# One lap loop for all rounds, the product with the one-hot columns behind the next step's sums, and the short block first, in a GNN layer on one Trainium2 core

## The chip, the cores and the metric

The kernel runs on one core of one Trainium2 chip. The metric is the device time of one execution in microseconds; the median of three runs is given. Engines are named as in the profile: PE (TensorE matmul), PEld (its weight loads), DVE (VectorE), ACT (ScalarE), POOL (GpSimd), SP (SyncE). q1 is the DMA queue that SP issues on, q10 the one of ACT.

## What is computed

```python
agg = segment_sum(edge_attr, dst, num_segments=6250)     # 200000 edges x 128 features, float32
h = relu(concatenate([x, agg, u[0]], axis=1) @ W1 + b1)  # x: 6250 x 128
y = x + h @ W2 + b2
out = (y - mean(y)) / sqrt(var(y) + 1e-5)                # by row
```

dst is sorted. The edges are 102 MB, x and the output 3.2 MB each.

## The kernel before

**Steps.** The edges are cut into 65 steps of 3072 (1.5 MB each), taken from the last to the first, plus a rest of 320 edges. Step t lands in one of 5 slots by one DMA on SP (line 304); SP issues load t when level1 of step t - 5 is done (level1_done). From t = DENSE = 30 on, a partition reads 12 edges in a row (wide form), before that 6.

**The sums of a step.** level1 (line 798) is 96 small products of PE: one-hot matrices `hot` (32 columns, made by DVE in make_hot, three steps ahead) times edges, into rows_ps, a PSUM buffer. ACT copies rows_ps to the SBUF buffer rows (copy_rows, line 412). level2 (line 815) multiplies rows by `row_hot`, a second one-hot matrix, into cols_ps; DVE adds cols_ps to agg_t at the step's base (add, line 602) and so frees the single cols_ps. There are three pairs of rows_ps and rows, used in the order SETS.

**The laps.** 5 steps are a lap, 13 laps in all, and a lap finishes one block of 512 nodes (the last of them 128 nodes, `final`). In laps 0 to 5 (sparse_lap) the columns are 224 and PE does level1(t), then level2(t - 1). In laps 6 to 12 (dense_lap) they are 128, and PE does level1(t), then level2(t), which waits for ACT's copy of the same step. These are two loops, with their own code on PE and DVE; SP, ACT and POOL are written out step by step.

**The block's layer.** For the block of lap l: turn_x (four transposes of x_rows into turn_ps, which is the same bank as hid_ps), copy_x (ACT), product1_x, product1_agg (after the last add of the lap), relu (ACT), product2, residual, variance, reciprocal_deviation (POOL), normalise, store. All but the turns come in the lap after. POOL's bias_add reads x_rows; then ACT issues the next x load. Block 11 (`short`) holds nodes 128 to 511 and the last 106 nodes, in three DMAs. In the last lap PE does a dummy product (line 903) ahead of level1(64).

**The judge.** In lap 8 DVE looks through all indices (judge, line 648), in lap 9 it makes `plan`, which says whether the general path must run.

## Time and profile before

| | us |
|---|---|
| median of three runs | 278.71 (277.7 to 279.08) |
| the profiled execution | 279.02 |
| its span | 277.3 |
| PE busy in the span | 215.6 (78%) |
| DVE busy | 168.1 (61%) |
| ACT busy | 51.3 (19%) |
| POOL busy | 41.5 (15%) |
| read from and written to memory | 106.63 MB, 3.20 MB |

The busy times are of one execution, taken by the hardware profiler; its own time stands beside its span. Ends of matmuls are modelled, so distances between starts say more than durations. A high busy share says nothing yet about who is waited for.

### The profile page before, as it was taken

The numbers are of one execution on the slowest core, as the hardware profiler recorded it, in microseconds if no ns is written. First come the engines' busy times: TensorE is split into PE (matmuls) and PEld (weight loads), VectorE is DVE, ScalarE is ACT, GpSimd is POOL, SyncE is SP. The second block draws the span as 40 slices with busy tenths as digits, with TensorE's granted clock in tenths as the row PEclk, the third lists the DMA queues.
The fourth block names the chain that finished last, engine by engine and source line by source line (L and its number), as shares of the span: only waits on it lengthen the run. The fifth ranks groups of instructions, "written<-read, shape, count | busy, mean of one in ns | idle before, by whom it ended". The sixth has DMA issues, their size and how long they took to land.

```text
span 277.3 us, 15287 instructions
## 1 busy us (share of the span) xinstructions
PE 215.6 (78%) x6763; PEld 171.2 (62%) x6763; DVE 168.1 (61%) x425; ACT 51.3 (19%) x100; POOL 41.5 (15%) x49
## 2 busy tenths in 40 slices
PE   0997599987776786796877599895897996867872
PEld 0895487856655665575556368674776675655751
DVE  7932475793774665665772526959938768464542
ACT  0511022311211210220210211322022122121210
POOL 6400020030210300400400300300304012030020
PEclk9999989999999999999995979999599999999998
DMA  7999999999999999999999999999999999999994
GB/s 248 351 386 400 401 398 400 401 401 402 402 399 402 402 400 401 402 400 412 417 412 409 416 414 418 414 417 416 417 415 418 414 419 414 409 423 410 420 399 175
DMA packets 30623, 110.06 MB, mean 397 GB/s; under 512 B 1976, under 2 KB 3150, under 8 KB 30606
## 3 DMA queue, kind: packets, MB, share of 16 engines
q1 hardware_dynamic: 27508, 105.83, 96.0%
q10 hardware_dynamic: 3098, 4.00, 4.1%
q8 instruction: 10, 0.16, 0.2%
q14 instruction: 7, 0.06, 0.1%
HBM read 106.63 MB, written 3.20 MB: 396 GB/s over the span
## 4 chain that ended last, share of the span: by engine, by line
PE 56%; DMA 18%; issue 15%; DVE 7%; POOL 1%; ACT 1%; DVEq 0%; POOLq 0%; ACTq 0%
PE rows_ps L810 30%; DMA slots<-in_edge_attr 18%; PE cols_ps L822 14%; PE hid_ps L854 3%; PE hid_ps L836 3%; PE hid_ps L845 2%; PE hid_ps L830 1%; ACT rows L418 1%; PE hid_ps L938 1%; DVE first_of_pair L540 1%; POOL rstd L382 1%; DVE dst_local L550 1%; DVE high L650 1%; DVE lowest L651 1%; DVE stats L630 1%
## 5 line engine op out<-in xcount | busy, mean ns | idle before, releaser
L810 PE MATMUL rows_ps<-slots,hot 64*32 64x128 f32 x6240 | 113.4, 287 | 34.3 <-issue 28.9
L810 PEld LDWEIGHTS rows_ps<-slots,hot 64*32 64x32 f32 x6240 | 94.4, 111 | 51.5 <-issue 49.6
L608 DVE TENSOR_TENSOR agg_t<-agg_t,cols_ps 128x128 f32 (+1 forms) x65 | 21.6, 332 | 94.8 <-PE cols_ps L822 94.7
L822 PE MATMUL cols_ps<-row_hot,rows 128*128 128x128 f32 (+1 forms) x260 | 56.8, 343 | 13.9 <-ACT rows L418 6.3
L582 DVE TENSOR_TENSOR hot<-edge_node,iota 128x768 f32<-128x768 f32 x65 | 61.9, 952 | 2.1 <-issue 1.8
L822 PEld LDWEIGHTS cols_ps<-row_hot,rows 128*128 128x128 f32 x260 | 41.2, 200 | 28.3 <-issue 15.1
L418 ACT ACTIVATE rows<-rows_ps 128x256 f32<-128x256 f32 x65 | 25.0, 384 | 179.4 <-PE rows_ps L810 175.4
L382 POOL TENSOR_TENSOR rstd<-var_eps,minus_half 128x4 f32<-128x4 f32 (+1 forms) x13 | 16.6, 1276 | 201.9 <-DVE var_eps L639 201.9
L598 DVE TENSOR_TENSOR row_hot<-row_node,iota 128x256 f32<-128x256 f32 (+1 forms) x65 | 38.5, 592 | 0.0
L373 POOL TENSOR_TENSOR z<-x_rows,b_all 128x512 f32<-128x512 f32 (+1 forms) x13 | 17.2, 1323 | 28.0 <-PE hid_ps L830 27.9
L645 DVE TENSOR_SCALAR z<-z,moments,rstd (+1 forms) x49 | 17.4, 412 | 1.1 <-POOL rstd L382 1.0
L438 ACT ACTIVATE x_t<-hid_ps 128x512 f32<-128x512 f32 (+2 forms) x13 | 13.1, 1011 | 8.4 <-PE hid_ps L830 8.4
L854 PE MATMUL hid_ps<-w_sb,hid 128*128 128x128 f32 x98 | 13.9, 283 | 0.5 <-ACT hid L449 0.5
L836 PE MATMUL hid_ps<-x_t,w1x 128*128 128x512 f32 (+1 forms) x26 | 13.4, 596 | 0.5 <-DVE agg_t L608 0.5
L854 PEld LDWEIGHTS hid_ps<-w_sb,hid 128*128 128x128 f32 x98 | 12.3, 191 | 2.0 <-issue 1.4
L449 ACT ACTIVATE hid<-hid_ps,bias 128x512 f32<-128x512 f32 (+2 forms) x13 | 8.5, 654 | 22.6 <-PE hid_ps L845 21.1
L845 PE MATMUL hid_ps<-agg_t,w1a 128*128 (+1 forms) x24 | 11.8, 574 | 0.5 <-DVE agg_t L608 0.5
L630 DVE BATCH_NORM_STATS2 stats<-z 128x6 f32 (+1 forms) x49 | 10.7, 279 | 0.0
L620 DVE TENSOR_TENSOR z<-z,hid_ps 128x512 f32 (+1 forms) x13 | 8.5, 653 | 1.6 <-PE hid_ps L854 1.6
L830 PE MATMUL hid_ps<-ident,x_rows 128*128 128x128 f32 x49 | 7.7, 276 | 0.8 <-issue 0.2
L845 PEld LDWEIGHTS hid_ps<-agg_t,w1a 128*128 128x128 f32 x24 | 4.4, 189 | 5.5 <-issue 4.7
L830 PEld LDWEIGHTS hid_ps<-ident,x_rows 128*128 128x128 f32 x49 | 5.7, 140 | 2.7 <-issue 2.4
(111 smaller groups left out, 65.6 us busy)
## 6 DMA issues: line engine op xcount, KB each, us to landing
slots<-in_edge_attr SPq DMA_DIRECT2D x65, 1536.0 KB, 17.3
x_rows<-in_x ACTq DMA_DIRECT2D x11, 256.0 KB
out<-z SPq DMA_DIRECT2D x11, 256.0 KB
dst_int<-in_dst SPq DMA_DIRECT2D x1, 384.0 KB, 3.8
dst_int<-in_dst ACTq DMA_DIRECT2D x1, 384.0 KB, 4.7
x_rows<-in_x ACTq DMA_DIRECT2D x1, 192.0 KB
out<-z SPq DMA_DIRECT2D x1, 192.0 KB
rest_slot<-in_edge_attr ACTq DMA_DIRECT2D x1, 160.0 KB, 8.8
```

The costliest lines, as they stand in the source:

```text
L373: G.tensor_tensor(z[:, bass.ds(i, 1), 0:m, :].rearrange("p o r f -> p (o r) f"), x_rows[:, 0:m, :], b2_all[:, :].unsqueeze(1).broadcast_to ...
L382: G.tensor_tensor(rstd[:, 0:m], var_eps[:, 0:m], minus_half[:, 0:m], ALU.pow).then_inc(rstd_made, 1)
L418: A.activation(rows[i][:, :, :], rows_ps[i][:, :, 0:feats], ACT.Copy).then_inc(rows_copied, 1)
L582: V.tensor_tensor(hot[i][:, :, :], edge_node[:, bass.ds(t, 1), :, :].rearrange("p o c r -> p (o c r)").unsqueeze(2).broadcast_to([P, RUNS, ...
L598: V.tensor_tensor(row_hot[i][:, :, 0:n], row_node[:, bass.ds(t, 1), :].rearrange("p o h -> p (o h)").unsqueeze(2).broadcast_to([P, HALVES, ...
L608: V.tensor_tensor(cols, cols, cols_ps[:, 0:n], ALU.add).then_inc(added, 1)
L645: done = V.tensor_scalar(row(i, r), row(i, r), moments[:, r, 0:1], rstd[:, r:r + 1], ALU.subtract, ALU.mult)
L810: done = T.matmul(rows_ps[i][c * SPAN:(c + 1) * SPAN, h, 0:feats], hot[j][part, c * RUN + r, :], slots[part, j, c, r * feats:(r + 1) * fea ...
L822: done = T.matmul(cols_ps[:, 0:n], rows[i][:, h, :], row_hot[j][:, h, 0:n], start=(h == 0), stop=(h == HALVES - 1))
L836: T.matmul(hid_ps[:, 0:n], w1x[:, :], x_t[:, 0:n], start=True, stop=False)
L845: done = T.matmul(hid_ps[:, 0:n], w1a[:, :], agg_t[:, bass.ds(at, n)], start=False, stop=True)
L854: done = T.matmul(y_ps[:, r, :], hid[:, r * P:(r + 1) * P], w2_sb[:, :], start=True, stop=True)
```

## The change

- One loop runs over laps 0 to 12 on PE and over laps 1 to 12 on DVE (lap 0 is written out there, and DVE's pass begins with the last step of the lap before). All steps but the last have 224 columns, and level2(t - 1) comes behind level1(t), except at j = 4 (the last step of a lap), where level2(t - 1) comes ahead of level1(t), because steps 3 and 4 of a lap use the same pair of buffers.
- There are two pairs of rows_ps and rows. The turned x gets a PSUM bank of its own (turn_bank), and the small products of the start move to it and to few_ps.
- product1_x moves from the start of the next lap to j = 4 of its own lap, behind turn_x (j = 3) and level2 of step 3. product1_agg is at j = 1, product2 at j = 2. turn_x and product1_x always take four tiles of rows.
- The blocks now begin at node 128. The first one is the short one (490 nodes, 122 partitions of four rows and one of two), in three DMAs; POOL zeroes x_rows before. The final block, nodes 0 to 127, stays last. The dummy product is gone.

```diff
--- before.py
+++ after.py
...
-SETS = (0, 1, 0, 1, 2)
-DENSE_LAP = 6
-DENSE = DENSE_LAP * LAP
+SETS = (0, 1, 0, 1, 1)
+DENSE = 6 * LAP
...
+    def start_of(i):
+        return 0 if isinstance(i, int) and i == final else FIRST + (blocks - 1) * BLOCK - i * BLOCK
+    def pieces_of(i, rows, home):
+        at = start_of(i)
+        if i == 0:
+            mid, low_end = at + top_even * ROWS, at + top_parts * ROWS
+            return ((rows[at:mid, :].rearrange("(p r) f -> p (r f)", r=ROWS), home(slice(0, top_even), ROWS)),
+                    (rows[mid:low_end, :].rearrange("(p r) f -> p (r f)", r=ROWS), home(slice(top_even, top_parts), ROWS)),
+                    (rows[low_end:nodes, :].rearrange("(p r) f -> p (r f)", r=top_rows), home(slice(top_parts, top_parts + 1), top_rows)))
+        if i == final:
+            return ((rows[0:FIRST, :], home(slice(0, P), 1)),)
+        return ((rows[at:at + BLOCK, :].rearrange("(p r) f -> p (r f)", r=ROWS), home(slice(0, P), ROWS)),)
...
-        rows_ps = [pb(f"rows_ps{i}", [P, HALVES, 512]) for i in range(3)]
+        rows_ps = [pb(f"rows_ps{i}", [P, HALVES, 512]) for i in range(2)]
         cols_ps = pb("cols_ps", [P, 512])
+        turn_bank = pb("turn_bank", [P, BLOCK])
         hid_ps = pb("hid_ps", [P, BLOCK])
+        few_ps = pb("few_ps", [P, 512])
         y_ps = hid_ps[:, :].rearrange("p (r f) -> p r f", r=ROWS)
-        turn_ps = y_ps
+        turn_ps = turn_bank[:, :].rearrange("p (r f) -> p r f", r=ROWS)
...
+            G.memset(x_rows[:, :, :], 0.0).then_inc(x_zero, 1)
...
             def load_x(seq):
-                i = seq % places
                 if seq:
                     act.wait_ge(z_ready, seq)
-                if i == short:
-                    act.dma_start(x_rows[:, 0:ROWS - 1, :].rearrange("p r f -> p (r f)"), x_second).then_inc(x_in, 16)
-                    act.dma_start(x_rows[0:last_even, ROWS - 1, :], x_last[0:last_even, :]).then_inc(x_in, 16)
-                    act.dma_start(x_rows[last_even:last, ROWS - 1, :], x_last[last_even:last, :]).then_inc(x_in, 16)
-                elif i == final:
-                    act.dma_start(x_rows[:, 0, :], x_first).then_inc(x_in, 16)
                 else:
-                    act.dma_start(x_rows[:, :, :].rearrange("p r f -> p (r f)"), x_full[blocks - 1 - i]).then_inc(x_in, 16)
+                    act.wait_ge(x_zero, 1)
+                for memory, home in pieces_of(seq % places, x, lambda parts, r: x_rows[parts, 0:r, :].rearrange("p r f -> p (r f)")):
+                    act.dma_start(home, memory).then_inc(x_in, 16)
...
-                dense_lap = lap >= DENSE_LAP
                 for j in range(LAP):
                     t = lap * LAP + j
-                    if dense_lap:
+                    if t:
                         copy_rows(t)
-                    elif t + 1 < DENSE:
-                        copy_rows(t + 1)
-                    if j == 0 and lap:
+                    if j == 1 and lap:
                         relu(lap - 1)
                     elif j == 3:
                         copy_x(lap)
...
+            def one_lap(lap):
                 at = counts(lap)
-                for j in range(LAP):
+                for j in range(-1, LAP - 1):
                     t = lap * LAP + j
-                    mixed = not isinstance(lap, int) and j + AHEAD >= LAP
-                    add(t, at[j], False)
-                    if not isinstance(lap, int):
-                        if j == 2:
-                            residual(lap - 1, lap - 1)
-                        elif j == 3:
-                            variance(lap - 1, lap - 1)
-                        elif j == 4:
-                            normalise(lap - 1, lap - 1)
-                    make_hot(t + AHEAD, j + AHEAD, None if mixed else False)
-            def dense_lap(lap):
-                at = counts(lap)
-                for j in range(LAP):
-                    t = lap * LAP + j
-                    add(t, at[j], True)
+                    add(t, at[j + 1], COLS)
                     if j == 1:
                         residual(lap - 1, lap - 1)
                         with dve.If(lap == JUDGE):
                     elif j == 3:
                         normalise(lap - 1, lap - 1)
                     if j + AHEAD < LAP:
-                        make_hot(t + AHEAD, j + AHEAD, True)
+                        make_hot(t + AHEAD, j + AHEAD)
                     else:
                         with dve.If(lap < laps - 1):
-                            make_hot(t + AHEAD, j + AHEAD, True)
+                            make_hot(t + AHEAD, j + AHEAD)
...
+            first_at = step_bases(0, LAP - 1)
+            for t in range(LAP - 1):
+                add(t, first_at[t], COLS)
+                make_hot(t + AHEAD, t + AHEAD)
+            dve.wait_ge(wide_ids_copied, SHARE)
             dve.wait_ge(first_in, 16)
             V.tensor_copy(edge_node[:, held, :, :].rearrange("p (b c) r -> p b (c r)", b=GROUPS), first_int[:, :, :])
-            with dve.Fori(DENSE_LAP, laps) as lap:
-                dense_lap(lap)
+            with dve.Fori(1, laps) as lap:
+                one_lap(lap)
+            add(held, 0, DENSE_COLS)
...
-            def turn_x(seq, i, landed):
+            def turn_x(seq, landed):
                 pe.wait_ge(x_in, landed)
-                pe.wait_ge(z_made, seq + 1)
-                for r in range(rows_of(i)):
+                for r in range(ROWS):
                     done = T.transpose(turn_ps[:, r, :], x_rows[:, r, :], ident[:, :])
                 done.then_inc(x_turned, 1)
-            def product1_x(seq, i):
+            def product1_x(seq, n):
+                pe.wait_ge(z_made, seq + 1)
                 pe.wait_ge(x_copied, seq + 1)
+                T.matmul(hid_ps[:, 0:n], w1x[:, :], x_t[:, 0:n], start=True, stop=False)
...
-            def sparse_lap(lap):
-                counts(lap)
-                for j in range(LAP):
-                    t = lap * LAP + j
-                    level1(t, lap, j)
-                    if j:
-                        level2(t - 1, j - 1, False)
-                    else:
-                        with pe.If(lap > 0):
-                            level2(t - 1, LAP - 1, False)
-                        with pe.If(lap < 1):
-                            first_products()
-                    if j == 1:
-                        with pe.If(lap > 0):
-                            finished(lap)
-                            product1_agg(lap - 1, start_of(lap - 1))
-                    elif j == 2:
-                        with pe.If(lap > 0):
-                            product2(lap - 1, lap - 1)
-                    elif j == 4:
-                        turn_x(lap, lap, lap * 16 + 16)
-            def dense_lap(lap):
+            def one_lap(lap):
                 counts(lap)
                 for j in range(LAP):
                     t = lap * LAP + j
                     if j == 4:
-                        with pe.If(lap == JUDGE + 1):
-                            pe.wait_ge(plan_made, 1)
-                        with pe.If(lap > final - 1):
-                            product1_x(final, final)
-                            pe.wait_ge(rows_copied, laps * LAP)
-                            T.matmul(rows_ps[SETS[j]][:, 0, feats:512], ident[:, :], iota[:, feats:512], start=True, stop=True)
+                        level2(t - 1, j - 1, COLS)
+                        product1_x(lap, BLOCK)
                     level1(t, lap, j)
                     if j == 0:
-                        finished(lap)
+                        with pe.If(lap > 0):
+                            level2(t - 1, LAP - 1, COLS)
+                        with pe.If(lap < 1):
+                            first_products()
                         with pe.If(lap == JUDGE + 1):
                             pe.wait_ge(bad_counted, 1)
                             T.matmul(bad_ps, bad_count[:, :], ones[:, 0:1], start=True, stop=False)
                             T.matmul(bad_ps, first_bad_count[:, :], ones[:, 0:1], start=False, stop=False)
                             T.matmul(bad_ps, rest_bad_count[:, :], ones[0:HALF, 0:1], start=False, stop=True).then_inc(bad_summed, 1)
-                        with pe.If(lap < final):
+                    elif j == 1:
+                        with pe.If(lap > 0):
+                            pe.wait_ge(added, lap * LAP + 1)
                             product1_agg(lap - 1, start_of(lap - 1))
-                        with pe.If(lap > final - 1):
-                            product1_agg(short, 0)
-                    elif j == 1:
-                        product2(lap - 1, lap - 1)
+                        level2(t - 1, j - 1, COLS)
+                    elif j == 2:
+                        with pe.If(lap > 0):
+                            product2(lap - 1, lap - 1)
+                        level2(t - 1, j - 1, COLS)
                     elif j == 3:
-                        with pe.If(lap < final):
-                            with pe.If(lap > short - 1):
-                                pe.wait_ge(x_in, x_landed(short))
-                            turn_x(lap, lap, lap * 16 + 16)
-                        with pe.If(lap > final - 1):
-                            turn_x(final, final, x_landed(final))
-                    level2(t, j, True)
+                        level2(t - 1, j - 1, COLS)
+                        turn_x(lap, lap * 16 + x_landed(0, 0))
...
-            with pe.Fori(0, DENSE_LAP) as lap:
-                sparse_lap(lap)
-            level2(DENSE - 1, LAP - 1, False)
-            with pe.Fori(DENSE_LAP, laps) as lap:
-                dense_lap(lap)
+            with pe.Fori(0, laps) as lap:
+                one_lap(lap)
+            level2(held, LAP - 1, DENSE_COLS)
...
```

## Rows read from the trace of the kernel before

**Rows 1.** The page's forty slices: busy tenths of the DMA engines.

```profile
DMA  7999999999999999999999999999999999999994
```

**Rows 2.** Tile slots, loads issued at 60-116, 164-169, 34-37 and 190-197.

```profile
DMA to landing us min/median/max: 18.3/18.5/18.6
...
DMA to landing us min/median/max: 9.3/9.3/9.4
...
DMA to landing us min/median/max: 13.5/13.5/13.5
...
DMA to landing us min/median/max: 13.7/13.7/13.7
```

**Rows 3.** Timeline, 101 to 134 us: start, us, engine, line, what.

```profile
101.16 1.02 PE L845 MATMUL hid_ps<-agg_t,w1a 128*128 x2
...
102.11 1.59 PE L810 MATMUL rows_ps<-slots,hot 64*32 64x128 f32 x96
...
103.64 1.02 PE L822 MATMUL cols_ps<-row_hot,rows 128*128 128x224 f32 x4
...
104.50 1.05 PE L854 MATMUL hid_ps<-w_sb,hid 128*128 128x128 f32 x8
...
132.16 1.02 PE L822 MATMUL cols_ps<-row_hot,rows 128*128 128x224 f32 x4
...
133.33 0.39 DVE L608 TENSOR_TENSOR agg_t<-agg_t,cols_ps 128x224 f32 x1 [1.73 <-PE cols_ps L822]
...
133.86 1.00 PE L822 MATMUL cols_ps<-row_hot,rows 128*128 128x224 f32 x4 [0.24 <-DVE agg_t L608]
```

**Rows 4.** Timeline of the tail, from add(62) to the last store.

```profile
263.86 0.29 DVE L608 TENSOR_TENSOR agg_t<-agg_t,cols_ps 128x128 f32 x1 [1.37 <-PE cols_ps L822]
...
264.70 1.58 PE L810 MATMUL rows_ps<-slots,hot 64*32 64x128 f32 x96 [0.98 <-issue]
...
265.70 1.02 POOL L382 TENSOR_TENSOR rstd<-var_eps,minus_half 128x4 f32<-128x4 f32 x1 [16.33 <-DVE var_eps L639]
...
267.84 1.11 DVE L645 TENSOR_SCALAR z<-z,moments,rstd  x4
...
268.41 1.58 PE L810 MATMUL rows_ps<-slots,hot 64*32 64x128 f32 x96
...
270.49 0.71 PE L822 MATMUL cols_ps<-row_hot,rows 128*128 128x128 f32 x4 [0.49 <-ACT rows L418]
271.34 0.29 DVE L608 TENSOR_TENSOR agg_t<-agg_t,cols_ps 128x128 f32 x1 [2.39 <-PE cols_ps L822]
...
275.29 0.36 SPq L318 DMA_DIRECT2D out<-z  x1
```

**Rows 5.** Timeline of PE in the first lap; instruction queue in 136 to 160 us.

```profile
32.76 0.54 PE L822 MATMUL cols_ps<-row_hot,rows 128*128 128x224 f32 x2 [2.83 <-issue]
...
q8 instruction: 4, 0.07, 1.1%
```

**Rows 6.** DMA packets in 261 to 262 and in 266.5 to 267.5 us.

```profile
DMA packets 76, 0.44 MB, mean 442 GB/s; under 512 B 4, under 2 KB 4, under 8 KB 76
...
DMA packets 217, 0.41 MB, mean 414 GB/s; under 512 B 25, under 2 KB 25, under 8 KB 217
```

**Rows 7.** Timeline of PE: level1(0).

```profile
12.49 2.81 PE L810 MATMUL rows_ps<-slots,hot 64*32 64x128 f32 x96
```

**Rows 8.** Timeline of PE in the first lap: level1(4).

```profile
33.23 2.61 PE L810 MATMUL rows_ps<-slots,hot 64*32 64x128 f32 x96
```

**Rows 9.** Timeline, lap 8: DVE after judge(), and level1(44).

```profile
191.32 0.96 DVE L582 TENSOR_TENSOR hot<-edge_node,iota 128x768 f32<-128x768 f32 x1
...
193.71 2.67 PE L810 MATMUL rows_ps<-slots,hot 64*32 64x128 f32 x96
```

**Rows 10.** A stretch: us; busy us by engine; PEclk, DMA share, GB/s.

```profile
272.00:276.00 4.00, 0.66 (x4) 0.30 (x2) 1.26 (x5) 0.37 (x1) 0.56 (x1) 0.98 0.35 125
```

**Rows 11.** The page: instruction queue q8, packets, MB, share.

```profile
q8 instruction: 10, 0.16, 0.2%
```

More of the change, by code:

```diff
@@ L61, in residual_gnn_layer @@
     blocks = nodes // BLOCK
-    last = nodes - blocks * BLOCK
-    last_even = last // 16 * 16
     chunks = blocks + 1
     laps = steps // LAP
-    width = max(nodes + COLS, chunks * BLOCK)
+    width = FIRST + chunks * BLOCK
+    top = nodes - FIRST - (blocks - 1) * BLOCK
+    top_parts, top_rows = top // ROWS, top % ROWS
+    top_even = top_parts // 16 * 16
     assert feats == P and GROUPS * (steps - 1) == P and TURNS == RUN // 2 and rest == HALF * rest_run and 0 < rest
-    assert steps == laps * LAP and DENSE_LAP + 1 < laps - 2
-    assert blocks == laps - 1 and 0 < last_even < last <= P and BLOCK - FIRST == P * (ROWS - 1)
+    assert steps == laps * LAP and blocks == laps - 1 and FIRST == P and nodes + COLS <= width
+    assert top_parts < P and 0 < top_even < top_parts and 0 < top_rows
     edge_steps = edge_attr[rest:edges, :].rearrange("(s c p r) f -> s p c (r f)", c=TILES, p=P, r=RUN)
@@ L156, in residual_gnn_layer @@
         row_hot = [sb(f"row_hot{i}", [P, HALVES, COLS]) for i in range(HOTS)]
-        rows = [sb(f"rows{i}", [P, HALVES, feats]) for i in range(3)]
+        rows = [sb(f"rows{i}", [P, HALVES, feats]) for i in range(2)]
         agg_t = sb("agg_t", [P, width])
@@ L295, in residual_gnn_layer, with x_landed @@
         pieces = places + 2
-        def x_landed(seq):
-            turns, i = seq // places, seq % places
-            return 16 * (turns * pieces + i + 1 + (2 if i >= short else 0))
+        def x_landed(turns, i):
+            return i * 16 + 16 * (turns * pieces + 3)
         @block.sync
@@ L573, in make_rows, with make_hot @@
                 dve.wait_ge(row_node_made, 1)
[L575 removed]
+            def make_hot(t, j):
                 i = j % HOTS
@@ L675, in counts @@
             def counts(lap):
-                for j in range(-1, LAP + AHEAD + 1):
+                for j in range(-2, LAP + AHEAD + 1):
                     dve.compute_val(lap * LAP + j)
@@ L813, in level1, with level2 @@
                 done.then_inc(level1_done, 1)
-            def level2(t, j, dense_step):
-                i, n = SETS[j], DENSE_COLS if dense_step else COLS
+            def level2(t, j, n):
+                i = SETS[j]
                 pe.wait_ge(rows_copied, t + 3)
```

111 lines of the change are left out of this document (31 added, 80 removed).

## The prediction

> **What bounds the kernel now.** I read the page's forty slices first. [rows 1]: the DMA row is 9 from the second slice to the last but one, so the sixteen DMA engines never pause; no engine's own row does that. Nearly all of it is the edge stream. So the end is set by the stream, which lands load 64 just before level1(64) starts at 268.41 [rows 4], and by what follows it. Busy time on PE, DVE or ACT counts only if it (a) lets the stream run dry or (b) lies between the last landings and the last store.
>
> How near the stream is to running dry is read from issue to landing [rows 2]. Well fed, a load takes 18.5 us, four others being queued ahead of it. Loads issued between 164 and 169 us took only 9.3 us, and the DMA row shows 9 all the same. So until that figure falls under 9.3 us, late releases of a slot cost nothing that this trace can show.
>
> The profiled run took 279.02 us: its span of 277.3 and 1.7 around it. The median is 278.71, 0.3 lower. I work on the profiled run and subtract 0.3 at the end.
>
> **The change part by part, in the steady stretch.** Laps 6 to 12 (35 steps) get 224 columns: level2 takes 1.02 us instead of 0.71, the add 0.39 instead of 0.29 [rows 3, 4]; PE has 35 x 0.31 = 11 us more, DVE 3.5 us more for the adds and, if row_hot grows by as much per column, some 7 us more for it (it has twice the columns). A lap of PE work by distances of starts [rows 3]: 5 x (1.53 + 0.86) for level1 and level2, 0.5 for the turns, 2 x 0.95 for product 1, 1.05 for product 2: 15.4 us, against 18.6 us for five landings (the last two level1 starts are 3.71 apart [rows 4]). PE keeps 3 us per lap, DVE more, and the stream hides this. In exchange PE no longer waits for ACT's copy between level1 and level2, 0.49 us in a dense step [rows 4]. That buys nothing either: PE was waiting for data.
>
> One loop instead of two takes away a first pass over new code. In the first lap PE stands for 2.83 us in the middle of a level2, waiting for nothing but issue; in the first dense lap q8, which moves instructions, has 4 packets in 136 to 160 us [rows 5]. At 1.1% of 16 engines over 24 us they are 4.2 engine-us, 1.06 us each, on one engine at a time. PE's stall is hidden; the DMA engine's time is the interesting part. At 261 to 262 us packets average 0.44 MB / 76 = 5.8 KB (edges). At 266.5 to 267.5 they are 217 packets of 0.41 MB; without the 25 tiny ones, 192 packets of 6 KB or 2 KB with that sum are 4 edge packets and 188 of out [rows 6]. Four packets of some 0.24 us are one engine: fifteen have finished load 64 and are already storing, and PE waits for the sixteenth. So not the mean load of the engines counts but that of the slowest, which trails by at least 1 us; I put its lead at no more than 1.7 us, since PE starts 1.9 us after 266.5. If the laggard is one of the four engines that the dense loop's code delayed, it comes 1.06 us earlier or more; if not, nothing is gained. Ends 0 and 1.7; nothing says which is nearer, I take the middle, 0.8.
>
> The Trainium skill, "Runtime: NRT & Kernel Launch", Instruction fetch mechanics, says that code comes in 16 KiB blocks which the sequencer prefetches through a DMA queue of its own; q8's 0.07 MB in 4 packets agrees [rows 5]. What it says on branches belongs to a rival, below.
>
> **The head.** The first x load becomes three DMAs on ACT's queue and waits for POOL's new memset of x_rows. Both lie before level1(0), which starts at 12.49, right behind PE's own transposes of the indices [rows 7]. The memset stands ahead of POOL's memsets of agg_t, which are needed only for the first add; ACT's two further issues (about 0.4 us each, as the store's issue in [rows 4]) push its copy of the first indices and so hot(0) by about 0.8 us, which DVE makes while PE transposes. Cost 0, at most 0.8.
> In the first lap level1(4) now stands behind turn_x, level2(3) and product1_x. It began at 33.23, PE being at half its clock there: level1 took 2.61 us instead of 1.58 [rows 8, 4]. I add 1.0 (turns) + 1.4 + 1.7, the distances 0.5, 0.86 and 0.95 nearly doubled: level1(4) begins at 37.3 and, at full clock again, ends at 38.9, 3.0 later than the 35.9 of before. Load 9 was issued then and took 13.5 us to land [rows 2]; it would take 10.5, still over 9.3. Cost 0, with 1.2 us left.
> The copies of steps 3 and 4 now go to one buffer, so PE must have level2(3) done before level1(4); ACT's copy of step 3 lies beside level2(2) and the turns.
>
> **The judge's lap.** judge() holds DVE until 191.32 [rows 9]. In the new order level2(43) waits for add(42) behind it, and queued behind level2(43) on PE are product 1, level1(44) and so the release of load 49. add(42) comes after judge() and one make_hot, about 192.8; + 0.53, level2(43); + 0.86 + 0.95, level1(44), which ends near 196.7. Before, it ended at 196.4, and its load took 13.7 us to land [rows 9, 2]. With the clock halved it ends near 199.2, and the load takes 10.9. Cost 0.
>
> **The tail carries the sum.** Before, PE was free between landings: level1(63) at 264.70, level1(64) at 268.41. Afterwards between these two stand level2(62), four turns instead of one, level2(63) and a product1_x of 512 columns instead of 128. By distances of starts [rows 3]: level1 to level2 1.53, so 266.23; its add starts 1.17 later, 267.40 (the turns, 0.86 + 0.5 behind level2, end before it); level2(63) starts 0.53 after the add, 267.93; + 0.86, product1_x 268.79; + 0.95, level1(64) at 269.74. That is 1.3 later. From there the chain is that of before: add + 2.93, last store + 6.88 [rows 4]. DVE has cover: from the add before the variance to the end of POOL's power are 2.86 us, so rstd is there at 267.40 + 2.86 + 0.1 = 270.4; normalise(11) (1.11, at most 1.5) ends by 271.9, and add(64) is due at 272.7. If that cover were gone, each us of lateness on DVE would be a us of the end. So the tail costs 1.3 us; bounds 0.8 (a semaphore step of 0.5 before level2(63) hidden) and 2.5 (half clock for level1(64), + 1.0). The stores behind load 64 are down to 125 GB/s in 272 to 276 [rows 10] and don't set the end.
>
> Sum: 279.02 + 1.3 - 0.8 = 279.5; less 0.3, 279.2 us.
>
> **The rivals.**
> First, full relief of the laggard: landing 1.7 earlier, everything else alike: 278.3. For it: fifteen engines are through; against: nothing shows which engines the four packets hit.
> Second, no relief: the laggard is another engine: 280.0.
> Third, slower by a dry stream at the start: a code stall of 2.8 us like the one in [rows 5] falls between turn_x and the end of level1(4), whose code now lies later. Load 9's 10.5 us become 7.7, 1.6 under the least value seen, so up to 1.6 us come on top: 280.8 to 281.6. It decides as soon as level1(4) ends after about 40.1. Against it: before, PE ran on from 33.23 without such a stall.
> Fourth, code fetched again in every lap: each jump back to the loop's start reloads blocks, PE stalls for some 2.8 us in each of 12 laps, the 3 us left per lap just keep the stream, and 12 x 1.06 engine-us fall on some engines: up to + 1, 280.2. The trace of before has ten such packets in all, loops included [rows 11], so 2 in 100. The page and section of the Trainium skill named above state this as a rule for a taken branch whose target lies outside the two pages held; this trace doesn't show it.
>
> **How the numbers follow.** A measurement can tell about 0.5%, 1.4 us, from no change: 277.3 to 280.1. Chances: forecast 0.42, full relief 0.18, no relief 0.16, dry start 0.16, code in every lap 0.02, others 0.06 (half of them faster). The forecast lies inside the 0.5% but for a sixth of its chance, no relief half, full relief but for a third. So faster 0.09, same 0.60, slower 0.31. The range goes from full relief less the 0.7 by which the runs differ, 277.6, to the dry start, 281.5.
>
> **What would show it.** Right: level1(64) starts 4.9 to 5.1 us after level1(63) instead of 3.7, and the last store as far behind level1(64) as before; the DMA row 9 throughout; four packets of q8 in the first lap and none near 136 to 160; no PE wait for ACT's copies in the later laps. Wrong: a slice under 9 near 40 to 45 or 200 us; issue to landing under 9.3 us; add(64) behind normalise(11).

## The result and the profile after

The kernel after takes 279.33 us (median of 19 runs, 278.99 to 279.59), the kernel before 278.71 (19 runs, 277.7 to 279.54): ratio 1.0029, interval 1.0021 to 1.0037. The forecast was 279.2 in 277.6 to 281.5, "same" the likeliest.

The page after: busy time by engine, the DMA row, the rate of each slice, and the queue that moves PE's code.
```profile
PE 224.6 (81%) x6762; PEld 171.9 (62%) x6762; DVE 181.8 (66%) x425; ACT 51.4 (19%) x98; POOL 38.2 (14%) x51
...
DMA  7999999999999999999999999999999999999994
GB/s 251 347 350 400 401 399 400 402 399 402 402 400 402 401 400 402 401 402 409 415 418 418 415 419 417 415 417 420 415 416 415 418 416 418 414 418 416 413 401 180
...
q8 instruction: 5, 0.08, 0.1%
```
PE has 9 us more work and DVE 14, and the DMA row is the one of before [rows 1]: the stream hides both. q8 has 5 packets where before had 10 [rows 11].

The end of the kernel after in order of time: start, us, line, operation, and in brackets the idle time before it and who ended it.
```profile
263.56 1.58 PE L778 MATMUL rows_ps<-slots,hot 64*32 64x128 f32 x96 [0.33 <-issue]
...
265.07 1.02 PE L790 MATMUL cols_ps<-row_hot,rows 128*128 128x224 f32 x4
...
265.93 0.60 PE L797 MATMUL turn_bank<-ident,x_rows 128*128 128x128 f32 x4
266.24 0.39 DVE L587 TENSOR_TENSOR agg_t<-agg_t,cols_ps 128x224 f32 x1 [0.48 <-PE cols_ps L790]
...
266.77 0.99 PE L790 MATMUL cols_ps<-row_hot,rows 128*128 128x224 f32 x4 [0.24 <-DVE agg_t L587]
...
267.60 1.02 PE L804 MATMUL hid_ps<-x_t,w1x 128*128 128x512 f32 x2
...
268.55 1.59 PE L778 MATMUL rows_ps<-slots,hot 64*32 64x128 f32 x96
...
269.23 1.25 DVE L624 TENSOR_SCALAR z<-z,moments,rstd  x4 [0.31 <-POOL rstd L389]
...
271.39 0.29 DVE L587 TENSOR_TENSOR agg_t<-agg_t,cols_ps 128x128 f32<-128x128 f32 x1 [0.91 <-PE cols_ps L790]
...
275.34 0.33 SPq L325 DMA_DIRECT2D out<-z  x1
```
Against [rows 4]: level1(63) starts 1.14 us earlier (263.56 for 264.70), level1(64) 0.14 later (268.55 for 268.41), the last store 0.05 later. The gap between the two level1 went from 3.71 to 4.99 us. The span is 277.3 us in both profiled executions.

Whether PE or the stream made level1 wait is told by when its load landed. Load 63 was issued at 247.2 us before and at 246.1 after; from issue to landing, before and after:
```profile
DMA to landing us min/median/max: 17.4/17.4/17.4
...
DMA to landing us min/median/max: 17.3/17.3/17.3
```
A load's semaphore is counted up sixteen times, once for each DMA engine, and the load is whole with the last of these updates. By them load 63 landed at 264.61 us before and at 263.47 after, and level1(63) starts 0.09 us behind it in both. Load 64 landed at 268.32 and 267.20; level1(64) starts 0.09 us behind it before and 1.35 us behind it after. So the stream brings the last loads 1.1 us earlier, and PE's work takes 1.3 us of that back.

What lies around the span is not the same. Over all its executions beside the kernels below the kernel before has a median span of 276.9 to 277.2 and 1.7 us around it; the kernel after 277.2 and 2.1. So of the difference of 0.62 us some 0.2 are inside the span and 0.4 outside.

### The profile page after: what moved, and what is told of

The parts are those of the page before. It is cut to its first block, busy times and chain, and to the rows that moved or that the text cites. A ratio compares the mean times of both kernels' runs of the same rounds, so it can differ in the third digit from the quotient of the medians.

```text
span 277.3 us, 15256 instructions
## 1 busy us (share of the span) xinstructions
PE 224.6 (81%) x6762; PEld 171.9 (62%) x6762; DVE 181.8 (66%) x425; ACT 51.4 (19%) x98; POOL 38.2 (14%) x51
## 4 chain that ended last, share of the span: by engine, by line
DMA 45%; PE 35%; DVE 10%; issue 7%; DVEq 1%; POOL 1%; ACT 1%; POOLq 0%
DMA slots<-in_edge_attr 45%; PE rows_ps L778 18%; PE cols_ps L790 8%; PE hid_ps L804 2%; PE hid_ps L808 2%; PE hid_ps L813 2%; DVE hot L573 1%; DVE row_hot L578 1%; PE hid_ps L866 1%; DVE z L624 1%; DVE agg_t L587 1%; DVE first_of_pair L531 1%; DVE dst_local L541 1%; DVE lowest L630 1%; DVE high L629 1%
## 5 line engine op out<-in xcount | busy, mean ns | idle before, releaser
L778 PE MATMUL rows_ps<-slots,hot 64*32 64x128 f32 x6240 | 108.0, 279 | 31.0 <-issue 18.4
L587 DVE TENSOR_TENSOR agg_t<-agg_t,cols_ps 128x224 f32 (+1 forms) x65 | 25.0, 384 | 79.8 <-PE cols_ps L790 78.9
L790 PE MATMUL cols_ps<-row_hot,rows 128*128 128x224 f32 x260 | 65.8, 377 | 8.3 <-DVE agg_t L587 7.8
L790 PEld LDWEIGHTS cols_ps<-row_hot,rows 128*128 128x128 f32 x260 | 46.4, 196 | 23.2 <-issue 18.9
L578 DVE TENSOR_TENSOR row_hot<-row_node,iota 128x448 f32<-128x448 f32 x65 | 52.0, 800 | 0.0
L804 PE MATMUL hid_ps<-x_t,w1x 128*128 128x512 f32 x26 | 15.8, 693 | 0.4
L439 ACT ACTIVATE x_t<-turn_bank 128x512 f32<-128x512 f32 (+1 forms) x13 | 13.4, 1027 | 12.9 <-PE turn_bank L797 12.9
L446 ACT ACTIVATE hid<-hid_ps,bias 128x512 f32<-128x512 f32 (+1 forms) x13 | 8.6, 662 | 11.7 <-PE hid_ps L808 11.7
L609 DVE BATCH_NORM_STATS2 stats<-z 128x6 f32 (+1 forms) x49 | 10.7, 280 | 0.0
L797 PE MATMUL turn_bank<-ident,x_rows 128*128 128x128 f32 x52 | 7.8, 273 | 0.0
L797 PEld LDWEIGHTS turn_bank<-ident,x_rows 128*128 128x128 f32 x52 | 6.5, 141 | 0.6
```

Of the source, the lines that this page charges most:

```text
L578: V.tensor_tensor(row_hot[i][:, :, :], row_node[:, bass.ds(t, 1), :].rearrange("p o h -> p (o h)").unsqueeze(2).broadcast_to([P, HALVES, C ...
L587: V.tensor_tensor(cols, cols, cols_ps[:, 0:n], ALU.add).then_inc(added, 1)
L778: done = T.matmul(rows_ps[i][c * SPAN:(c + 1) * SPAN, h, 0:feats], hot[j][part, c * RUN + r, :], slots[part, j, c, r * feats:(r + 1) * fea ...
L790: done = T.matmul(cols_ps[:, 0:n], rows[i][:, h, :], row_hot[j][:, h, 0:n], start=(h == 0), stop=(h == HALVES - 1))
L797: done = T.transpose(turn_ps[:, r, :], x_rows[:, r, :], ident[:, :])
L804: T.matmul(hid_ps[:, 0:n], w1x[:, :], x_t[:, 0:n], start=True, stop=False)
```

## Experiments

All times are medians; "span" is the median span. The kernel before ran beside each and took 278.6 to 278.9 us.

**1. What the gap before level1(64) costs.** Three kernels change only the work that stands there. The first is the kernel after, with the last product1_x behind level1(64) and 128 columns wide:
```diff
-                        product1_x(lap, BLOCK)
+                        with pe.If(lap < final):
+                            product1_x(lap, BLOCK)
                     level1(t, lap, j)
+                    if j == 4:
+                        with pe.If(lap > final - 1):
+                            product1_x(final, P)
```


> The changed kernel, but in the last lap product1_x stands behind level1(64) and takes 128 columns. Theory (the added time is PE work between level1(63) and level1(64)): the distance of their starts falls from 5.0 to 4.1 us (product1_x takes 0.95 us of it), the product hides beside ACT's copy of step 64, and the time falls by 0.9 us against the changed kernel's 279.33, to 278.4, so at or just under the kernel before. Rival (the added time comes from the head or the steady stretch): the distance falls but the last data comes later anyway, so 279.3.

Measured: 278.53 us (278.18 to 278.75), ratio to before 0.9994 [0.9984, 1.0005], span 276.4. The same rows of its trace:
```profile
263.42 1.58 PE L778 MATMUL rows_ps<-slots,hot 64*32 64x128 f32 x96 [0.29 <-issue]
...
266.63 1.00 PE L790 MATMUL cols_ps<-row_hot,rows 128*128 128x224 f32 x4 [0.24 <-DVE agg_t L587]
...
267.55 1.59 PE L778 MATMUL rows_ps<-slots,hot 64*32 64x128 f32 x96
...
269.08 0.49 PE L804 MATMUL hid_ps<-x_t,w1x 128*128 128x128 f32 x2
```
The gap falls from 4.99 to 4.13 us and the time by 0.80. Load 64 landed at 267.06, so level1(64) still starts 0.49 us behind it. The other two go the other way, from the kernel before, which has one dummy product there:
```diff
                             T.matmul(rows_ps[SETS[j]][:, 0, feats:512], ident[:, :], iota[:, feats:512], start=True, stop=True)
+                            T.matmul(rows_ps[SETS[j]][:, 0, feats:512], ident[:, :], iota[:, feats:512], start=True, stop=True)
+                            T.matmul(rows_ps[SETS[j]][:, 0, feats:512], ident[:, :], iota[:, feats:512], start=True, stop=True)
```


> The kernel before with three dummy products instead of one ahead of level1(64), 1.4 us more of PE work in the gap between the last two level1. Theory (PE work between the last two landings comes straight onto the end once the gap is full): level1(64) starts 5.0 to 5.2 us after level1(63) instead of 3.7, the time goes from 278.7 to 280.0, less by as much as PE had room (0.1 us in the trace). Rival (some wait of the tail other than PE's order sets the end): 278.7.

> The kernel before without the dummy product. Theory: level1(64) starts when its data is there, and the dummy ended 0.06 us before, so 278.7 or at most 0.3 us less (in runs in which the data comes early, PE was held up by the dummy). Rival (the dummy is itself the end of the gap in most runs): 0.7 us less, 278.0, and level1(64) starts less than 3.6 us after level1(63). A second rival (the dummy keeps the clock up): a lower granted clock behind 268 us and a longer time.

Three dummies: 279.86 us, ratio 1.0038 [1.002, 1.0057]; level1(64) starts 4.88 us after level1(63):
```profile
264.51 1.58 PE L810 MATMUL rows_ps<-slots,hot 64*32 64x128 f32 x96 [0.98 <-issue]
...
268.65 0.81 PE L905 MATMUL rows_ps<-iota,ident 128*128 128x384 f32 x2
...
269.39 1.59 PE L810 MATMUL rows_ps<-slots,hot 64*32 64x128 f32 x96
```
No dummy: 278.62 us, ratio 0.9995 [0.9984, 1.0005]; gap 3.72 us. In the two, level1(64) starts 1.26 and 0.09 us behind the landing of load 64. So work on PE that reaches beyond the last landing counts in full (+1.17 us of gap, +1.25 of time), and work that ends ahead of it counts nothing: the change crosses from the second to the first. The second rival's lower clock shows without the dummy only behind 272 us (0.74 granted in 272 to 277, 0.89 in the kernel before), and the last store still comes 6.89 us behind level1(64): it costs nothing here.

**2. A second loop's code.** The kernel after, its PE loop written twice, with the same steps in it:
```diff
-            with pe.Fori(0, laps) as lap:
+            with pe.Fori(0, 6) as lap:
+                one_lap(lap)
+            with pe.Fori(6, laps) as lap:
                 one_lap(lap)
```


> The changed kernel with its lap loop written twice on PE, for laps 0 to 5 and 6 to 12; the same work in the same order. Theory (instruction packets delay single DMA engines, and the slowest engine sets the landings): four or five more packets of q8 near 136 to 160 us, PE stalls of 2 to 3 us there, level1(63) starts up to 1.1 us later than in the changed kernel (263.6), the time is 0 to 1.3 us longer than 279.33, and single runs differ by over 1 us instead of 0.6. Rival (code loading is hidden altogether): the same stalls, level1(63) where it was, 279.3, runs within 0.6.

Measured: 282.87 us (281.13 to 283.91), ratio 1.015 [1.0124, 1.0176], far beyond what was expected. PE stands for instructions four times by over 1 us in the second loop's first pass (1.41, 1.51, 2.29 and 2.62 us), and the stream runs dry. The two long stalls; then stretches with the busy us of PE, PEld, DVE, ACT, POOL, the granted clock, the DMA share and GB/s; then q8 in 134 to 170 us:
```profile
153.27 0.64 PE L778 MATMUL rows_ps<-slots,hot 64*32 64x128 f32 x25 [2.29 <-issue]
...
162.80 0.43 PE L778 MATMUL rows_ps<-slots,hot 64*32 64x128 f32 x10 [2.62 <-issue]
```
```profile
162.00:164.00 2.00, 0.64 (x23) 0.41 (x30) 0.49 (x1) 0.38 (x1) 0.00 (x0) 1.00 0.79 326
164.00:166.00 2.00, 2.00 (x99) 1.80 (x90) 0.00 (x0) 0.38 (x1) 0.00 (x0) 1.00 0.89 245
```
```profile
q8 instruction: 4, 0.07, 0.8%
```
The shortest time from issue to landing there is 7.1 us, and level1(63) starts at 265.45, 1.9 late. The landings are 0.3 us ahead of those of the kernel after until the dry stretch, 0.3 behind them after it, and 1.6 behind them after a fifth block of code at 182.9 us (experiment 5 has the same step in the kernel before). So the dry stretch is the smaller part of the 1.9 us. The profiled execution is the fastest of the six (281.13); what makes the median 1.7 us longer no trace shows. As the stream also ran dry, the run is no clean test of the slowest DMA engine. It says that one loop is the safer form: in this order a first pass over new code in mid-stream costs 3.5 us of time.

**3. 224 columns without the new order.** The kernel before, with 224 columns in laps 6 to 12 too:
```diff
-                    n = DENSE_COLS if dense_step else COLS
+                    n = COLS
...
-                i, n = SETS[j], DENSE_COLS if dense_step else COLS
+                i, n = SETS[j], COLS
```


> The kernel before with 224 instead of 128 columns in level2, row_hot and the add of the last seven laps, nothing else. Theory (the stream hides the wider columns except behind level1(64)): the last level2 and the last add take 0.3 and 0.1 us longer, so 0.4 us more than before's 278.6, 279.0. Rival (the wider columns are what made the changed kernel slower): PE and DVE lag behind the stream through the dense laps, whose code loading already brought loads down to 9.3 us from issue to landing, the stream runs dry near 165 us, and 279.6 or more. The theory has this as its own risk: dry if issue to landing falls under 8.7 us.

Measured: 281.07 us, ratio 1.009 [1.0057, 1.0122], span 279.35: the hidden-columns theory missed by 2 us here. Two stretches of its trace, and one of issue to landing for the loads of 196 to 206 us:
```profile
202.00:204.00 2.00, 2.00 (x82) 1.68 (x83) 2.00 (x4) 0.00 (x0) 0.00 (x0) 0.86 0.98 329
...
212.00:220.00 8.00, 6.11 (x245) 4.75 (x229) 6.96 (x21) 2.23 (x4) 2.93 (x2) 1.00 0.99 394
```
```profile
DMA to landing us min/median/max: 8.7/8.8/8.9
```
Before has 413 GB/s in 202 to 204 and 417 in 212 to 220. level1(63) starts at 265.99, 1.29 later than in [rows 4]. Load 63 landed at 265.30, 0.69 later than in the kernel before, and PE began 0.69 behind it instead of 0.09: the stream and PE are both late. So the columns are hidden in the kernel after, but not by the 3 us of the prediction alone. The likely reason is the order: in the old one level2 stands right behind level1 of its own step and waits for ACT's copy (0.49 us, as in [rows 4]), and the 0.31 us of the wider columns come on top; the new order takes this wait away in the same laps. That is argued; no run changed the wait alone.

**4. The judge's lap.** The kernel after, with judge()'s two long reductions done twice (3.4 us more on DVE, no result changes):
```diff
-                V.tensor_reduce(high[:, :], dst_int[:, :, :], AX.X, ALU.max)
-                then(V.tensor_reduce(lowest[:, :], dst_int[:, :, :], AX.X, ALU.min))
+                for _ in range(2):
+                    then(V.tensor_reduce(high[:, :], dst_int[:, :, :], AX.X, ALU.max))
+                    then(V.tensor_reduce(lowest[:, :], dst_int[:, :, :], AX.X, ALU.min))
```


> The changed kernel with judge()'s two large reductions done twice, 3.5 us more of DVE in lap 8, and a wait between them. Theory (late releases cost nothing until issue to landing comes under the 8.7 us of the very first load, then us for us): the load issued at 199.6 us is issued 3.5 us later, its 9.6 us to land would be 6.1, so the stream is dry for 2 to 3 us near 205 us and the time is 281.3 to 282.3. Rival (a deep queue hides a delay of this size): 279.3.

Measured: 281.15 us, ratio 1.0085 [1.0062, 1.0109], span 278.65. In the 4 us shown, the sixteen DMA engines stand for 1.6 us on the mean, which is how much later level1(63) starts (265.16):
```profile
202.00:204.00 2.00, 1.48 (x88) 1.24 (x80) 2.00 (x7) 0.38 (x1) 0.00 (x0) 0.91 0.40 163
204.00:206.00 2.00, 2.00 (x100) 1.80 (x84) 0.56 (x2) 0.38 (x1) 0.00 (x0) 1.00 0.80 173
```
```profile
DMA to landing us min/median/max: 7.2/8.0/8.8
```
So of 3.4 us more on DVE 1.8 were swallowed; the shortest time from issue to landing in that lap of the kernel after is 9.6 us. The landings moved by 1.3 us there, and the spread, the time between the first and the last of the sixteen engines to finish one load, shrank from 2.2 to 0.8 us: the engines that were ahead ran dry first. The time is a little under the 281.3 to 282.3 expected.

**5. The slowest DMA engine.** Four small extra loads in laps 6 to 9, once as one row (one packet of 16 KB, 0.62 us on one engine), once over 16 rows of 1 KB as a control:
```diff
+                    if j == 1 and lap in (6, 7, 8, 9):
+                        if lap > 6:
+                            act.wait_ge(extra_in, 16 * (lap - 6))
+                        act.dma_start(extra[:, :], edge_attr[0:32, :].rearrange("(a e) f -> a (e f)", a=1)).then_inc(extra_in, 16)
```


> The changed kernel with four extra loads of 16 KB into one partition, on ACT's queue in laps 6 to 9; one descriptor each, so each on one DMA engine, 0.6 to 0.7 us of it at the 25.7 KB per us that an edge packet shows. Theory (the slowest engine sets the landings): if all four fall on one engine, it loses 2.5 us; the others had a spread of up to 2.3 us at the last load, so level1(63) starts 0.2 to 2.5 us later than 263.6 and the time is 279.5 to 281.8. Rival (only the bytes in total count): 64 KB are 0.16 us, 279.5.

> The control of the run before: extra loads of the same number, at the same places, but 16 partitions of 1 KB, spread over all engines. Both theories: 0.16 us for the bytes, 279.4 to 279.5, level1(63) within 0.2 us of 263.6.

Measured: 279.94 and 280.03 us, spans 277.55 and 277.75. The control is no faster than the test, so by their times the pair tells nothing apart. level1(63) comes 0.17 and 0.56 us later than in the kernel after, where 0.16 was expected of the control: the control missed. The next pair adds code instead: waits on a semaphore long reached, in POOL's written-out order, 80 in each of 13 places, then in the first 11 places only.
```diff
                 if i + 1 < places:
                     bias_add(i + 1, i + 1)
+                for _ in range(80):
+                    pool.wait_ge(half_made, 1)
```


> The kernel after, with 80 more waits in each of the 13 places of POOL's written-out order, all on a semaphore that has long been reached: 1040 instructions that do nothing but have to be loaded, on an engine that is idle over 200 of 277 us. Nothing is added on PE, DVE, ACT or the stream. The theory (what the kernel after gained before level1(63) is the one DMA engine that no longer carries four blocks of code): four to five more q8 packets show, spread over the laps, level1(63) starts 0.7 to 1.2 us later than after's 263.56, and the time is 280.0 to 280.5 us. The rival (level1(63) came earlier for another reason, such as loads that are issued sooner in the steady laps): q8 has its nine or ten packets and the time stays at 279.3 us. If q8's packets do not become more, the run tells nothing.

> As e10_pool_code, but without the 80 waits in the last two places. In e10 level1(63) started at 264.37 us, 0.81 later than in the kernel after, which is what the theory of the one DMA engine had said, but POOL still had 80 waits before it behind the last rstd, and the program ended 3.6 us behind the last normalise where after's ends 2.0 behind it: 1.6 us of the 3.0 that e10 lost are that tail of POOL's own. With 880 waits in places 0 to 10 the theory expects three to four more blocks of code than after, level1(63) at 264.2 to 264.5 us, the end of the program 2.0 to 2.4 us behind the last normalise, and 279.9 to 280.3 us. The rival (the blocks cost nothing, and e10's later level1(63) was what a single execution varies by): level1(63) at 263.6 to 263.9 and 279.3 us.

Measured: 282.3 us (ratio 1.0124 [1.0106, 1.0143]) and 280.27 us (1.0051 [1.0037, 1.0064]), spans 280.25 and 278.0. In the first the span ends 4.1 us behind the last normalise (2.0 in the kernel after): 2.1 us are POOL's own last 80 waits. q8 keeps its 5 packets, the case in which the first of the pair was to tell nothing; the added code shows on queue q14 instead, in blocks of 8 KB (6 packets in the kernel after). q14's row and level1(63) of the first, then of the second:
```profile
q14 instruction: 10, 0.08, 0.1%
```
```profile
264.37 1.58 PE L780 MATMUL rows_ps<-slots,hot 64*32 64x128 f32 x96 [0.33 <-issue]
```
```profile
q14 instruction: 9, 0.07, 0.1%
```
```profile
264.02 1.58 PE L780 MATMUL rows_ps<-slots,hot 64*32 64x128 f32 x96 [0.34 <-issue]
```
What the blocks did is seen in the landings of the loads. Against the same load of the kernel after, in us (minus is earlier):
```
landed in the kernel after at     90.5   177.7   182.1   185.9   209.2   263.5
before                           -0.53   -0.66   +0.64   +0.98   +0.99   +1.14
before, three dummies            -0.62   -0.67   +0.24   +0.83   +0.85   +0.96
before, no dummy                 -0.58   -0.73   +0.39   +0.92   +0.92   +1.05
loop written twice               -0.25   +0.19   -0.40   +1.64   +1.59   +1.89
80 waits in 13 places            -0.28   -0.41   +0.29   +0.30   +0.27   +0.81
80 waits in 11 places            -0.02   -0.14   -0.06   -0.05   -0.05   +0.46
extra loads of one row           -0.14   -0.12   -0.11   -0.11   -0.09   +0.17
extra loads of 16 rows            0.00   +0.23   +0.24   +0.40   +0.40   +0.57
```
Single landings beside a load of x swing by some tenths; what stays from one load to the next counts. Before is 0.5 to 0.7 us ahead until 177.7 us and loses 1.6 in the next two landings. There stands a fifth block of the second loop's code, at 179.1 us, 1.1 us long; the four in 136 to 160 (138.0, 144.2, 150.4, 156.7) cost nothing. The row of before for 178 to 182 us:
```profile
q8 instruction: 1, 0.02, 1.7%
```
One engine falls behind alone: the last two engines finish load 41 at 177.05 and 177.08 us and load 42 at 180.97 and 182.74. The spread is 2.3 us ahead of the block and 3.9 to 4.6 from there to the end, 3.6 to 4.2 in the two kernels of experiment 1 made from the kernel before, and 2.2 to 3.0 in the kernel after. The step is longer than the block's record of 1.1 us; what the other 0.5 us are is open. The blocks of q14 do the same on a smaller scale: those at 62, 79 and 118 us cost nothing, the one at 177 (0.31 us long) cost 0.6 us in one kernel and nothing in the other, the one at 238 0.6 and 0.5. Of the one-row loads three cost nothing and the fourth, at 209 us, 0.3. The 16-row loads cost 0.1 to 0.2 us each, wherever they stand. So a block of code seems to delay the end only if it falls on the engine that is already last, or makes its engine the last: before paid once, for the fifth block. The records do not name a packet's engine, so this is inferred from the landings.

**6. The first x load.** Between 14 and 17 us the kernel after moves less than before. The three stretches after (before has 362, 387 and 380 GB/s; in 12 to 14 us both are slow, 278 GB/s before and 265 after):
```profile
14.00:15.00 1.00, 1.00 (x56) 1.00 (x45) 1.00 (x3) 0.00 (x0) 0.00 (x0) 1.00 1.02 268
15.00:16.00 1.00, 1.00 (x27) 0.60 (x11) 0.97 (x6) 0.34 (x1) 0.00 (x0) 1.00 1.04 290
16.00:17.00 1.00, 1.00 (x5) 0.92 (x4) 0.34 (x4) 0.05 (x1) 0.00 (x0) 1.00 1.01 331
```
A kernel issues that load at 13.3 us instead of 6.4; it stands on the version of the next paragraph.
```diff
-            load_x(0)
             act.dma_start(first_int[:, :, :], dst_first).then_inc(first_in, 16)
...
                 copy_wide_ids(k)
+            load_x(0)
             copy_rows(0)
```


> As e9_two_cols, and the first load of x (three pieces in the kernel after) is issued behind the copies of the wide indices, at about 14 us, where it was at 6.4 us. It tests why the stream carries less between 14 and 17 us in the kernel after (268, 290 and 331 GB/s in the three microseconds) than in the kernel before (362, 387, 380). The theory (the x load beside the stream makes every packet take longer): 12 to 14 us shows over 350 GB/s, the slow stretch stands behind the new issue, and the time moves by 0.3 us at most, since the same work is only done later. The rival (the small packets of first_int, or the edge stream's own start, make it): the stretch stays where it is and ends with first_int's packets.

Its stretches:
```profile
14.00:15.00 1.00, 1.00 (x56) 1.00 (x48) 1.00 (x3) 0.39 (x1) 0.00 (x0) 1.00 1.02 360
15.00:16.00 1.00, 1.00 (x41) 0.61 (x25) 1.00 (x3) 0.00 (x0) 0.00 (x0) 1.00 1.08 405
...
17.00:20.00 3.00, 3.00 (x21) 2.71 (x28) 0.00 (x0) 0.34 (x2) 0.00 (x0) 1.00 1.04 343
```
From 14 us on the slow stretch has moved behind the new issue, as the theory says; 12 to 14 us stayed slow (260 GB/s), which it did not say, so the x load is not the only cause. In the profiled executions the stream keeps a lead of 0.3 us over the version without the move to the end (level1(63) at 263.23 for 263.55), yet the median is 278.41 us against 278.33 without the move: no gain that can be told. Why the stream of before, whose x load is issued at 6.5 us too, is back at 362 GB/s by 14 us is open.

**7. The version with both orders mended.** The kernel after with the edit of the first experiment, and a second PSUM place for the column sums of the step with j = 3, so that level2(63) does not wait for add(62) (PE also waits for the plan in lap 9 again, as in the kernel before):
```diff
+        cols_of = [few_ps[:, 256:256 + COLS] if j == 3 else cols_ps[:, 0:COLS] for j in range(LAP)]
...
-                pe.wait_ge(added, t + 1)
+                pe.wait_ge(added, t if j == 3 else t + 1)
```


> The kernel after, with two changes of the tail's order. The last lap's product of the short place (256 to 128 columns) stands behind level1(64), as in e1_product_behind, and the column sums of the step with j = 3 get a second PSUM place (the free columns 256 to 479 of few_ps), so that level2(63) does not wait for add(62). The theory (the gap between level1(63) and level1(64) is the work that stands between them and its one wait for an add): of e1's gap of 4.13 us the 0.24 us wait and some issue go, the gap becomes 3.7 to 3.9 us, and the time is 0.2 to 0.4 us under e1's: 278.2 us, ratio to before 0.998 to 0.999. The rival (the add's wait was covered by the landing of the last load, which then is what level1(64) waits for): the gap and the time stay at e1's 278.5 us.

Measured: 278.33 us (277.96 to 278.58, 12 runs), ratio to before 0.9986 [0.9974, 0.9997], span 276.2:
```profile
263.55 1.58 PE L779 MATMUL rows_ps<-slots,hot 64*32 64x128 f32 x96 [0.33 <-issue]
...
266.36 0.92 PE L791 MATMUL few_ps<-row_hot,rows 128*128 128x224 f32 x4
...
267.28 1.58 PE L779 MATMUL rows_ps<-slots,hot 64*32 64x128 f32 x96
```
The gap is 3.73 us, that of the kernel before, and this version beats both, by 1.0 us the kernel after, by 0.4 the kernel before. Load 64 landed at 267.18, 0.10 us ahead of level1(64): PE's order costs nothing any more. In the judge's lap the same edit lets level1(44) start at 193.14 us instead of 197.35, and the shortest time from issue to landing from there on is 10.7 us instead of 9.6. Against the kernel before the median span is 0.8 us shorter, and 0.3 more outside it take part of that back.

## Why the prediction was right, step by step

- **The steady stretch, cost 0.** Right in the result (no slice under 9 between the first and the last, PE +9 us, DVE +14). The reason was incomplete: I wrote that the wait for ACT's copy, once gone, buys nothing. In the old order 224 columns cost 2.4 us (experiment 3), so the new order buys the room for them, most likely by that wait. One sign was only half kept: between 130 and 262 us PE still waits for ACT's copies three times, 1.6 us in all, ahead of level1; before it was eleven times and 5.3 us, ahead of level2.
- **row_hot on DVE.** The growth per column was right: 0.62 us for 448 elements where 256 take 0.41, 7.4 us in 35 steps. Not foreseen is the rest (row_hot went from 38.5 to 52.0 us in all), told in the last section.
- **The laggard, 0.8 us of 0 to 1.7.** level1(63) came 1.14 earlier. The mechanism was right, the block was wrong: of the second loop's five blocks the fifth, outside the stretch I read, cost 1.6 us, and the four that I priced cost nothing. Against the 1.6 stand 0.6 lost at the start (experiment 6); 0.1 more falls to before near 240 us, unexplained. PE's start adds nothing, it is 0.09 us behind the landing in both. The 0.8 was the middle between two bounds and no price of its own; that it missed by 0.3 only is luck.
- **The tail, +1.3 us.** Right: the gap was to be 5.04 us and is 4.99; 1.28 late, and from there the last store at +6.79 where +6.88 was taken. normalise(11) ended at 270.5, add(64) began at 271.4: DVE's cover held. Experiment 1 shows the price one for one.
- **The head.** level1(4) was to begin at 37.3 and end at 38.9; it began at 38.02 and ended at 39.7. A stall for instructions of 3.11 us stood before it, where before had 2.83 [rows 5]:
```profile
32.73 0.29 PE L778 MATMUL rows_ps<-slots,hot 64*32 64x128 f32 x1 [3.11 <-issue]
...
36.18 1.91 PE L804 MATMUL hid_ps<-x_t,w1x 128*128 128x512 f32 x2
...
38.02 1.65 PE L778 MATMUL rows_ps<-slots,hot 64*32 64x128 f32 x96
```
 Load 9 landed 10.3 us after its issue (10.5 forecast): the third rival was 0.4 us from its point of decision. That point was set too early: in the kernels of experiment 1 (product behind), 5 (80 waits in 13 places) and 6 load 9 was issued at 41.2, 41.4 and 40.8 us and landed after 8.7, 8.4 and 8.9 us, and no later landing moved. level1(0) began 0.25 later. The first load landed when it did before, the second 0.66 later (16.68 for 16.02), and some 0.6 of this stayed. Cost 0 was wrong by that.
- **The judge's lap.** The granted clock was 0.54 from 194 to 199 us, so the slower of the two cases came: level1(44) ended at 199.5 (199.2 forecast). The load was issued at 199.6 and landed in 9.6 us instead of 10.9, at 209.2 where it had landed at 210.1: the stream was by then 1.0 us further on than I had counted, so that the same release came nearer to its edge.
```profile
193.89 1.83 PE L790 MATMUL cols_ps<-row_hot,rows 128*128 128x224 f32 x4 [4.97 <-DVE agg_t L587]
...
197.35 2.18 PE L778 MATMUL rows_ps<-slots,hot 64*32 64x128 f32 x96
```
- **Code in every lap (2 in 100).** q8 has 5 packets for 12 jumps back. The rule named for it (the Trainium skill, "Runtime: NRT & Kernel Launch", Instruction fetch mechanics) did not act on PE's loop here.
- **The sum.** For the span I had 277.3 + 0.5 = 277.8 and it is 277.3 (277.2 over all executions); 0.3 of the miss is the laggard's 1.14 for 0.8, 0.1 the last store's 6.79 for 6.88. What lies around it I had left at 1.7 and it is 2.1. Two misses of 0.5 and 0.4 us nearly cancel; 279.2 against 279.33 looks better than the steps were. Every version of the kernel after has 2.0 to 2.5 around its span, every version of the kernel before 1.7 to 1.8. The cause is open: no run tried it.

## What to carry to other kernels

When a stream sets the time, an instruction added near its end costs nothing or all of itself, and which of the two is decided by where it stands against the last landing: list what lies between the last two uses of the stream and move everything else behind them. Price the steady part by how long before the stream needs it a buffer is given back (issue to landing), in the worst lap, not by the mean idle time per lap; and read beside it how far the first and the last DMA engine are apart, since that takes up part of a dry stretch. And compare spans as well as whole times: a part of a difference can lie outside what the profile shows.

## What the runs showed of the hardware

- **The edge of a dry stream** is not one number here. A load that landed 8.3 us after its issue moved no later landing (168.7 us in the kernel without the dummy). At 8.7 us around 41 us (experiment 1, product behind) the rate fell to 346 GB/s for 2 us, the spread went from 2.1 to 1.7 us, and the landings stayed. At 7.1 and 7.2 us, with 245 and 163 GB/s, the landings moved by 0.6 and 1.3 us. But at 7.0 us (203.8 us with the loop written twice), with 133 GB/s, they did not move, and the spread went from 2.3 to 0.5 us. What a late release costs also depends on how far the last engine trails.
- **DVE beside POOL.** Once per lap row_hot takes 1.7 us instead of 0.62, and its mean goes to 800 ns. It is the one that stands beside POOL's add of x and the bias:
```profile
152.53 1.34 POOL L380 TENSOR_TENSOR z<-x_rows,b_all 128x512 f32<-128x512 f32 x1
152.65 1.71 DVE L578 TENSOR_TENSOR row_hot<-row_node,iota 128x448 f32<-128x448 f32 x1
...
156.47 0.61 DVE L578 TENSOR_TENSOR row_hot<-row_node,iota 128x448 f32<-128x448 f32 x1
```
 It ends 0.49 us after POOL's instruction does, as if it had hardly begun before. The Trainium skill, "SBUF — State Buffer", SBUF: two separate sides, says that the two engines share a port pair by an exclusive lock held for a whole instruction, where DVE's operation has two inputs in SBUF and POOL's reads SBUF, as here; this trace agrees. The kernel before has the same in its dense laps (1.51 us instead of 0.42), and hardly in the others. Some 13 us of DVE's time go there, all hidden by the stream.
- **One slow engine of sixteen** sets when a load is whole: a packet of 1.1 us on one engine went with every later landing being 1.6 us later for the remaining 80 us, while the mean of the sixteen engines moved by 0.1 us. The stream never gave it back.
- **From run to run.** Runs of the kernel before differ by 1.8 us, runs of the kernel after by 0.6, those of its version in experiment 6 by 2.1. Why is open.
